# Two recurrences on one Trainium2 core: the order of the triangles on GpSimd and ScalarE, and where TensorE writes an offset

## The reference, cut to what matters

```python
N, T, D, H = (64, 64, 128, 128)          # here 8 rows, 128 steps, width 128
xw = jnp.einsum('ntd,dh->nth', x, Wx) + b
def step(prev_h, xw_t):
    next_h = jnp.tanh(xw_t + prev_h @ Wh)
    return (next_h, next_h)
_, hs = jax.lax.scan(step, h0, jnp.swapaxes(xw, 0, 1))
```

## Time and profile before

| | us |
|---|---|
| median of 3 runs | 3132.15 |
| lowest, highest | 3104.95, 3172.81 |
| profiled execution, its time | 3091.48 |
| its span, first to last instruction | 3089.3 |
| TensorE busy in it | 2769.1 |
| VectorE busy | 2652.7 |
| GpSimd busy | 2224.6 |
| ScalarE busy | 1981.7 |

### The profile page before, as it was taken

How to read it: one execution, slowest core, us unless ns; L and a number is a source line. 1 busy time by engine, 2 the same in 40 slices (tenths; PEclk the granted TensorE clock), 3 DMA queues, 4 the chain that set the end, 5 groups by cost and what they waited for, 6 DMA issues and landing times.

```text
span 3089.3 us, 51130 instructions
## 1 busy us (share of the span) xinstructions
PE 2769.1 (90%) x12721; PEld 1526.5 (49%) x12721; DVE 2652.7 (86%) x7086; ACT 1981.7 (64%) x4426; POOL 2224.6 (72%) x2418
## 2 busy tenths in 40 slices
PE   5888888988989889888888888776999999999997
PEld 2343444433434434334433433663666666666665
DVE  4888988989998888898888999656899999999995
ACT  2555555555555555555555555345888888888886
POOL 5766766776776667666676676106999999999994
PEclk9999988999999999999999999998999999999998
DMA  5333333333333333333333333200001010101000
GB/s 133 76 74 68 75 62 68 74 72 73 72 73 74 69 68 74 70 75 68 73 72 73 68 75 75 86 1 1 1 0 39 0 39 0 39 0 39 0 0 8
DMA packets 368013, 163.07 MB, mean 53 GB/s; under 512 B 285158, under 2 KB 298220, under 8 KB 367212
## 3 DMA queue, kind: packets, MB, share of 16 engines
q1 hardware_dynamic: 367980, 162.65, 24.4%
HBM read 156.81 MB, written 5.80 MB: 53 GB/s over the span
## 4 chain that ended last, share of the span: by engine, by line
POOL 33%; issue 22%; PE 21%; DVE 15%; ACT 4%; POOLq 2%; DMA 1%; SPq 1%; DVEq 0%; ACTq 0%
DVE bank L1118 13%; POOL qkv_w L646 9%; POOL qk L719 7%; PE bank L1498 5%; PE bank L1483 5%; POOL qT L639 4%; POOL qkv_w L648 4%; PE bank L1478 3%; POOL rs L728 3%; POOL kT L639 2%; POOL qk L734 2%; ACT bank L807 2%; PE bank L1494 2%; ACT bank L812 1%; POOL rs L727 1%
## 5 line engine op out<-in xcount | busy, mean ns | idle before, releaser
L639 POOL TENSOR_TENSOR kT<-upto,xT 128x512 f32<-128x512 f32 x260 | 270.7, 1042 | 572.2 <-PE bank L1483 572.1
L1118 DVE TENSOR_REDUCE bank<-bank 128x4 f32<-128x1536 f32 x256 | 442.6, 1762 | 115.4 <-PE bank L1478 71.3
L1114 DVE TENSOR_REDUCE bank<-qkv_w 128x4 f32<-128x1536 f32 x256 | 449.4, 1756 | 48.8 <-ACT qkv_w L817 48.1
L1498 PE MATMUL bank<-qT,wh 128*128 128x256 f32 (+1 forms) x768 | 348.4, 537 | 78.5 <-POOL qT L639 48.2
L795 ACT ACTIVATE b<-bank,offset 128x512 f32<-128x512 f32 x258 | 177.3, 687 | 368.1 <-PE bank L1483 368.1
L1478 PE MATMUL bank<-diag_x,w_part 128*128 128x512 f32 x1032 | 386.8, 496 | 10.7 <-DMA diag_x<-diag_ring 10.7
L1478 PE MATMUL bank<-diag_h,w_part 128*128 128x512 f32 x1024 | 393.0, 504 | 0.2 <-DVE bank L1108 0.2
L1483 PE MATMUL bank<-kT,wx 128*128 128x512 f32 x516 | 288.1, 641 | 116.5 <-DVE bank L1118 116.5
L653 POOL TENSOR_TENSOR diag_h<-eye,part 128x512 fp32r<-128x512 f32 x384 | 389.0, 1042 | 0.0
L728 POOL TENSOR_TENSOR rs<-rs,halfs 128x8 f32<-128x8 f32 x192 | 368.4, 1919 | 16.0
L817 ACT COPY qkv_w<-bank 128x512 f32<-128x512 f32 x258 | 222.6, 863 | 203.1 <-PE bank L1478 203.1
(11 more groups left out here) (236 smaller groups left out, 6426.6 us busy)
## 6 DMA issues: line engine op xcount, KB each, us to landing
diag_x<-diag_ring SPq DMA_DIRECT2D x259, 512.0 KB, 6.1
qkv_w<-in_L_ffn_Wqkv SPq DMA_DIRECT2D x6, 1536.0 KB
diag_ring<-X SPq DMA_DIRECT2D x264, 4.0 KB, 5.3
diag_ring<-o_fin SPq DMA_DIRECT2D x8, 512.0 KB, 7.9
o_w<-in_L_ffn_Wo SPq DMA_DIRECT2D x6, 512.0 KB
w<-in_L_ffn_W SPq DMA_DIRECT2D x6, 341.0 KB
b<-in_L_ffn_b SPq DMA_DIRECT2D x6, 341.0 KB
w<-in_L_ffn_W SPq DMA_DIRECT2D x6, 128.0 KB
```

The lines of the kernel that those rows point to most:

```text
L639: pool.tensor_tensor(tri[n][:, rows, :], upto[:].unsqueeze(1).to_broadcast([P, 4, D]), src[:, rows].unsqueeze(2).to_broadcast([P, 4, D]), ...
L1114: return dve.tensor_reduce(minus_h[half][:, :, D - 1], chain[:, rows, :], AX_X, ALU.add)
L1118: return dve.tensor_reduce(pre[:, 4 * half:4 * half + 4], links_h[half], mybir.AxisListType.XY, ALU.add)
L1498: return pe.matmul(bank[:, GUESS_BANKS_H[half], (a - 4 * half) * D:(b - 4 * half) * D], wh[:], tri[0][:, a:b, :].rearrange("p n k -> p (n ...
```

## The change

Three edits in the loop of time steps.

1. GpSimd writes x's triangles for step t+1 (before: for t+2), and waits for the sums of the step's own counts (before: for those that TensorE makes in this same step). The pair for step 1 ahead of the loop goes.
2. ScalarE's `place_rests_x(1)` stands behind the next step's `triangle_mid`, and once behind the loop (before: at the end of the step).
3. `offset_h` takes one half, and is called three times for each half right behind that half's `sums_x` (before: once for both halves at the end of the step). The write has start=True, so it leaves the same 12 each time.

```diff
@@ GpSimd
             place_sums_x(1, 2)
-            for half in range(2):
-                triangle(1, xT[:, 1, :], half, tri_x)
             with pool.Fori(0, T) as t:
...
-                later = at_step(value(pool, t + 2))
+                later = at_step(this)
                 for half in range(2):
-                    pool.wait_ge(sum_ready[1], counts[2 + half])
+                    pool.wait_ge(sum_ready[1], counts[half])
                     triangle(1, later, half, tri_x)
@@ ScalarE
             place_rests_x(0, 1)
-            place_rests_x(1, 2)
...
                 triangle_mid()
+                place_rests_x(1, counts[1])
                 copy_guess_h(0, counts[0])
...
                 place_rests_x(0, counts[2])
-                place_rests_x(1, counts[3])
+            place_rests_x(1, 2 * T + 2)
@@ TensorE
-            def offset_h():
-
-                for which in GUESS_BANKS_H:
-                    pe.matmul(bank[:, which, :], offset16[:, 0:D], offset16[:, 2 * D:], start=True, stop=True,
-                              skip_group_check=True)
+            def offset_h(half):
+
+                pe.matmul(bank[:, GUESS_BANKS_H[half], :], offset16[:, 0:D], offset16[:, 2 * D:], start=True, stop=True,
+                          skip_group_check=True)
...
-            offset_h()
+            for half in range(2):
+                offset_h(half)
...
                     sums_x(half, counts[2 + half])
+                    for again in range(3):
+                        offset_h(half)
                 for half in range(2):
                     rests_x(half, counts[2 + half], landed)
-                offset_h()
```

## The result

| | before | after |
|---|---|---|
| median of 4 runs, us | 3118.55 | 2944.74 |
| lowest, highest | 3103.71, 3172.81 | 2943.41, 2948.01 |
| profiled execution, its time | 3091.48 | 2948.01 |
| its span | 3089.3 | 2945.8 |

The ratio is 0.947, with a 95% interval of 0.9414 to 0.9525: 5.3% faster; it is taken over the runs that lie within 1.5% of their kernel's fastest, where the medians by themselves give 0.944. The forecast was 2946. The runs of the changed kernel lie within 4.6 us of each other, those of before within 69 us.

What follows compares the result with a forecast made beforehand. The prediction took a chain of waits through GpSimd, beside VectorE, and clock falls to bound the loop: 3091.5 - 86.9 (shorter steps) - 58.8 (falls) = 2945.8, forecast 2946 us. Its own range was 2920 to 2975, with rivals 2920 to 3010.

Steps and rivals of the forecast that it cites:

- Sum: Profiled execution: 3091.5 less 86.9 us for shorter steps and 58.8 for clock falls gives 2945.8; forecast 2946 us, chance 0.64.
- Part 1: GpSimd: x's triangles move behind h's diagonals, new wait costs nothing; h's second triangle starts at 0.2 instead of 1.65 us.
- Part 2: ScalarE: h's triangles go ahead of x's second rests; TensorE's third half product starts 0.22 us earlier, at 1.11.
- Part 3: Chain of waits after both reorderings: folds of h end at 8.65 us, gain 0.69 us a step, step 13.60 us.
- Part 4: TensorE: three offset writes for each half leave it full but not late; cost 0.0 us, between 0.0 and 0.4.
- rival (b): TensorE becomes the bound, or L803 comes late: 0.2 to 0.4 us a step, 2984 us; chance 0.12.
- Part 5: Clock: a step's opening loses its waits and gets full-width products earlier, so no fall is left: 58.8 us gained.
- Rival (a): Clock falls stay, since waits removed are short and added writes use a single row: 3005 or 3046 us; chance 0.12.
- Rival (c): Slower: single-row writes in the step's middle become the new empty stretch, each step falls: 3296 us; chance 0.05.
- Rival (d): VectorE still held by minus_placed or the last diagonals; only 0.21 us a step comes back: 3006 us; chance 0.07.
- The median of before: Median 3132.15 us lies 40.7 above the profiled execution: what 15 more steps of 17.07 instead of 14.29 us would give.

Runs made afterwards that it cites:

- pool_alone: GpSimd's edit alone (x's triangles one step ahead) on the kernel before; 2972.70 us.
- before_full_rows: The kernel before with the offset written from 128 rows of weights of 1/128 in place of one row of 1; 3018.34 us, ratio 0.9775.
- writes_alone: The kernel before with only the three offset writes for each half, triangles and rests in the old order; 3109.32 us.
- five_writes: The changed kernel with five single-row offset writes for each half instead of three; 3155.24 us, ratio 1.0216 to the kernel before.
- act_alone: ScalarE's edit alone (x's second rests placed behind the next step's middle triangle) on the kernel before; 3110.20 us.

## Why the prediction was right, point by point

- *Sum.* Right: on the profiled execution 3091.5 - 84.4 - 58.8 = 2948.3 against 2948.0 measured; the forecast had 86.9 for the first term.
- *The step as a whole.* Step by step the runs add up: 14.29 - 0.46 (GpSimd) - 0.39 (ScalarE beside it) + 0.17 (the writes) = 13.61, against 13.62 measured.
- *Part 1, GpSimd.* Right, and shown by `pool_alone`. The new wait cost nothing, and h's triangle came at 0.16 (0.2 forecast).
- *Part 2, ScalarE.* The order came out as forecast (the moved copy 1112.24 to 1113.10, L801 0.32 us later). The worth of the edit, 0.22 us by itself, is wrong as a number of its own: nothing alone, 0.39 beside GpSimd's, 1.30 with the writes. The prediction didn't see that the writes without it would have made the kernel slower than its ordinary step, since it moved both at once.
- *Part 3, the chain.* Right to 0.02 us: L801 at 2.18 (2.17), L1105 at 2.80 (2.79), the folds from 5.24 to 8.67 (5.22 to 8.65), step 13.62 (13.60). The number is luck. TensorE started h's products 0.33 us later than forecast (0.80, not 0.47), because of the writes, and then took 0.95 us for the four half-width ones instead of 1.28. The pitch of 0.32 had been read from pairs that start behind a wait, and only their first gap is that long; the next are 0.22. The two errors cancel to the hundredth. Without the writes the first product does start 0.46 us after the triangle, and the step is 13.45, not 13.60: the gain of parts 1 and 2 was put 0.15 us too low, the cost of part 4 0.17 too low.
- *Part 4, the writes.* This is the step that failed: "full but not late: 0.0 us". They cost 0.17 us a step, 22 us. The first sums and writes took 1.80 us instead of 1.63, so the second sums started at step time 8.94, not 8.78; from there to the next h product it was 5.49 us (1106.55 to 1112.04), not 5.29, nearly all of it in the second sums and writes, 1.80 and not 1.63. TensorE was free at 14.43, not 14.07. The cause is the change from 128 rows to one and back, 0.3 us, of which the prediction had 0.1. The bounds, 0 to 0.4 us, held it. What stands in for VectorE as the bound is TensorE: rival (b) was partly true, hidden in the sum by part 3's pitch. What was held against it, that pitches are steady over the step, is not so: 0.32 and 0.22 us for the same product.
- *Part 5, the clock.* Right that no fall is left, and GpSimd's edit alone suffices. It takes the 0.40 us wait away and brings full-width work into the opening at once, so it doesn't show which of the two does it. That the waits as such do it, which the part also says, is not so: `before_full_rows` has them both and `writes_alone` has one of 1.02 us, and neither falls.
- *Rival (a).* Didn't happen, but its observation was the right one: nothing showed that single-row writes hold the clock up, and with 128 rows in their place it stays up. The Trainium skill, "TensorE: Matmul & The Clock Gate" (section Why this matters for your kernels), has a long idle gap between bursts lower the clock. The trace of `five_writes` disagrees once more: the clock falls 58 times, each time behind at least 4.2 us in which TensorE was busy throughout.
- *Rival (c).* Didn't happen with three writes and did with five, behind the writes, in 58 of 126 steps. How near three are to it was not tried (four weren't run). What was held against it was misread: in the kernel before, the two waits of the middle (0.34 and 0.55 us) are together longer than the opening's (0.17 and 0.40), not nearly as long, and yet no fall started there. That already spoke against waits as the cause.
- *Rival (d).* Didn't happen: the folds of h follow fold_x at once (1101.08 + 1.75 to 1102.85).
- *The median of before.* The 41 us above the profiled execution were put down to more falls. For the runs behind that median no clock is on record, so it stays argued; the kernel before's runs beside the experiments bear it out (0.961 to 0.962 at 3091 to 3094 us, 0.944 at 3136).

## What to carry to other kernels

When an in-order queue is relieved, look at what each engine's queue would hold with the edits one by one: an edit can look worthless alone and be needed beside another, as ScalarE's was. Work written to fill a gap in TensorE must be priced with the change of kind on both sides of it, and with the next engine's slack, which all such fills share. If TensorE's clock falls although it is hardly ever idle, try the filler with all rows of the array before adding more of it.

## What the runs showed of the hardware that was not expected

- The clock of TensorE fell to half behind a stretch where TensorE was busy throughout with sums and single-row writes (`five_writes`, 58 falls, at least 4.2 us without a pause ahead of each), and did not with the same instructions from 128 rows. In the kernel before, 128 rows in place of one in four writes a step took the falls from 34 stretches to none.
- Going from 128-row products to single-row ones and back cost 0.3 us: sums with five full-row writes took 1.93 us to the rests (1137.56 to 1139.49), sums with three single-row ones 1.80 (1106.55 to 1108.35).
- Half-width products that follow each other without a wait start 0.22 us apart, and the single-row write 0.31 behind the last, which makes 0.95 for four; where a wait stands ahead of a pair, its two start 0.32 apart.
- Falls can follow each other from step to step: in `act_alone` 60 steps in a row took 17.1 us.
